# Transposing fetches of the experts' token rows, woven back from two planes of 16-bit halves

## The reference

```
o = (silu(x @ gate_e.T) * (x @ up_e.T)) @ down_e.T      # 256 -> 128 -> 256 channels
out = x2 + gb * (sum over the 6 experts of weight * o  +  a shared expert of width 256)
```

## Time and profile before

| | us |
|---|---|
| median of 3 runs (lowest, highest) | 1335.8 (1335.38, 1337.43) |
| the profiled execution's own time | 1335.87 |
| its span, first to last instruction | 1334.1 |
| TensorE busy in the span | 1283.5 |
| VectorE busy | 1070.0 |
| ScalarE busy | 759.0 |
| GpSimd busy | 650.2 |

### The profile page before, as it was taken

How to read it: one execution, slowest core, us unless ns; L and a number is a source line. 1 busy time by engine, 2 the same in 40 slices (tenths; PEclk the granted TensorE clock), 3 DMA queues, 4 the chain that set the end, 5 groups by cost and what they waited for, 6 DMA issues and landing times.

```text
span 1334.1 us, 26082 instructions
## 1 busy us (share of the span) xinstructions
PE 1283.5 (96%) x8098; PEld 637.6 (48%) x8098; DVE 1070.0 (80%) x2592; ACT 759.0 (57%) x1093; POOL 650.2 (49%) x964
## 2 busy tenths in 40 slices
PE   9996999999999999999999999999999999999895
PEld 6652322333323323323333232558888888885441
DVE  6878999999999999999999996475444566665497
ACT  4553777777676776777677768314444444446100
POOL 1004123335655755656466557756766655564100
PEclk8996999999999999999999999999999999999998
DMA  6777555534347256264363453768776665554798
GB/s 219 242 232 192 148 154 109 96 74 115 88 110 172 54 136 143 68 144 111 93 162 80 145 183 101 244 220 264 235 218 201 192 185 183 183 172 131 292 327 322
DMA packets 215235, 224.81 MB, mean 169 GB/s; under 512 B 109926, under 2 KB 177142, under 8 KB 214972
## 3 DMA queue, kind: packets, MB, share of 16 engines
q1 hardware_dynamic: 188524, 150.22, 41.9%
q0 software_dynamic: 21152, 66.10, 14.1%
q10 hardware_dynamic: 5424, 6.82, 1.5%
HBM read 127.33 MB, written 95.70 MB: 167 GB/s over the span
## 4 chain that ended last, share of the span: by engine, by line
PE 69%; DVE 10%; DMA 4%; POOL 4%; SPq 2%; issue 1%; ACT 1%; ACTq 0%; DVEq 0%; POOLq 0%
PE psO L1381 14%; PE psE L1368 13%; PE psM L1358 9%; PE ex_psGU L1969 7%; PE ex_psGU L2030 7%; DVE piece_max L1236 6%; PE ex_psY L2050 4%; PE ex_psY L1979 3%; DMA wide<-results 2%; PE psM L576 2%; PE ex_psX L2016 2%; PE ex_psX L1957 2%; SPq L144 2%; PE co_psS L2446 1%; PE psGU L1721 1%
## 5 line engine op out<-in xcount | busy, mean ns | idle before, releaser
L1236 DVE TENSOR_REDUCE piece_max<-psM 128x1 f32<-128x512 f32 x1008 | 631.0, 682 | 20.0 <-PE psM L1358 16.5
L1319 ACT ACTIVATE wide<-psE 128x1024 f32<-128x1024 f32 x512 | 497.1, 1021 | 186.9 <-PE psE L1368 184.6
L1368 PE MATMUL psE<-wide 49*128 49x512 bf16 (+1 forms) x2048 | 327.3, 379 | 5.0 <-DMA wide<-maxima 4.7
L1358 PE MATMUL psM<-wide 48*128 48x512 bf16 x1008 | 312.0, 389 | 11.7 <-DVE piece_max L1236 11.5
L1381 PE MATMUL psO<-wide 128*32 128x512 f32 x2048 | 273.2, 606 | 0.6 <-ACT wide L1319 0.6
L2261 POOL DMA_INDIRECT results<-vals_inv,places x208 | 200.3, 963 | 127.7 <-DVE vals_inv L2142 104.5
L1358 PEld LDWEIGHTS psM<-wide 48*128 48x128 bf16 x1008 | 76.4, 93 | 322.9 <-DVE piece_max L1236 271.4
L1368 PEld LDWEIGHTS psE<-wide 49*128 49x128 bf16 (+1 forms) x2048 | 118.0, 95 | 94.5 <-issue 11.9
L1455 POOL DMA_INDIRECT lists<-last_rows,slot x96 | 93.8, 977 | 52.6 <-issue 22.3
L1455 POOL DMA_INDIRECT lists<-rows,slot x96 | 94.6, 986 | 49.4 <-PE psO L1381 26.4
L2030 PE MATMUL ex_psGU<-wide,ex_xT 128*128 (+1 forms) x416 | 107.8, 382 | 0.8 <-ACT h2T L2103 0.8
(11 more groups left out here) (349 smaller groups left out, 1570.8 us busy)
## 6 DMA issues: line engine op xcount, KB each, us to landing
wide<-qk_parts SPq DMA_DIRECT2D x384, 64.0 KB, 2.7
wide<-results SPq DMA_DIRECT2D x16, 1536.0 KB, 9.8
qk_parts<-parts SPq DMA_DIRECT2D x32, 384.0 KB, 2.7
rows<-lists SPq DMA_DIRECT2D x26, 320.0 KB
h2Ts<-lists SPq DMA_DIRECT2D x26, 320.0 KB
xin<-in_x_dram SPq DMA_DIRECT2D x16, 512.0 KB, 4.0
wide<-in_guT_dram SPq DMA_DIRECT2D x3, 2560.0 KB, 9.9
rows<-lists SPq DMA_DIRECT2D x44, 160.0 KB
```

What stands on the lines that cost most here:

```text
L1236: v.tensor_reduce(piece_max[:, qh, (x * PAIRS + h) * KT // QH + qt, kh:kh + 1], bank_of("piece", PIECES * group + n), AX.X, ALU.max, negat ...
L1319: nc.scalar.activation(probs[:, step % 2, 2 * pair:2 * pair + 2], psE[:, pair], ACT.Exp, scale=HD ** -0.5).then_inc(exp_ok, 1)
L1358: nc.tensor.matmul(bank_of(*user), qa[g][rows, h, qt * P:(qt + 1) * P], ka[g][rows, h, kh * 512:(kh + 1) * 512], start=True, stop=True).th ...
L1368: mm = nc.tensor.matmul(psE[:, pair, x], k[g][part, pair, kt * P:(kt + 1) * P], q[g][part, pair, qh * 512:(qh + 1) * 512], start=(q is qa) ...
```

## The change

1. `env.lists` keeps each token's 256 channels as two planes of 16-bit halves: 256 upper halves, then 256 lower halves. ScalarE makes them per chunk with two copies of 128x1024 16-bit elements (`planes`, at w = `SPLIT` = 25 of the window, and once in the closing stage); the normalised tokens stay in `env.xhat`, from which `turn_half` now reads. GpSimd's scatter waits for `planes_ok`, and SyncE's next load of values into the same memory waits for the transposes and the planes.
2. In the expert stage SyncE fetches the planes with a transposing DMA (`dma_start_transpose`), so that channels lie on partitions, and the 64 words of weights and positions with a plain DMA behind it: two transfers for each pair or tile, four for a mixed tile.
3. TensorE's transposes of rows (`turn_pair`, and those of `body`) are gone, and `ex_psX` with them.
4. The halves are woven into `ex_xT` by copies whose output steps over every second 16-bit place. In pairs ScalarE writes the upper halves and VectorE the lower ones (128x512 each); for single and mixed tiles ScalarE writes both (two of 128x256).
5. SyncE waits for the weaving (`x_ok`, `low_ok`) where it waited for the transposes (`x_done`).

The core of the diff:

```
-PROJECT, TURN, GATE, PLACE = 11, 21, 23, 28
+PROJECT, TURN, GATE, SPLIT, PLACE = 11, 21, 23, 25, 28
...
+def planes(act, env, c):
+    act.wait_ge(env.h2_ok, c + 1)
+    if c > 1:
+        act.wait_ge(env.scattered[(c - 2) % CPB], 16 * TPC * TOPK * ((c - 2) // CPB + 1))
+    halves = env.xhat.bitcast(U16).rearrange("p i (d h) -> p i d h", h=2)
+    to = env.rows_of(c)[:, :, 0:D].bitcast(U16)
+    env.nc.scalar.activation(to[:, :, 0:D], halves[:, :, :, 1], ACT.Copy)
+    env.nc.scalar.activation(to[:, :, D:2 * D], halves[:, :, :, 0], ACT.Copy).then_inc(env.planes_ok, 1)
...
-                    wait(sp, env.h2_ok, c)
+                    wait(sp, env.turned, KC * c)
+                    wait(sp, env.planes_ok, c)
...
             def scatter_step_by_step(c):
+                pool.wait_ge(env.planes_ok, c + 1)
...
             def pair_of_tiles(t, u, row):
-                wait(sp, x_done, t - DEEP + 2)
+                wait(sp, x_ok, t - DEEP + 2)
+                wait(sp, low_ok, min(t - DEEP + 2, SURE))
                 wait(sp, dest_ok, t - DEEP + 2)
-                sp.dma_start(pair_rows[u // 2], env.lists[bass.ds(row, 2 * P)].rearrange("(j p) n -> p j n", p=P)
+                sp.dma_start_transpose(pair_planes[u // 2], in_planes[bass.ds(row, 2 * P), 0:2 * D]).then_inc(rows_in[u], 16)
+                sp.dma_start(pair_marks[u // 2], env.lists[bass.ds(row, 2 * P), D:ROW].rearrange("(j p) n -> p j n", p=P)
                              ).then_inc(rows_in[u], 16)
...
-                for half, row in enumerate(both):
-                    sp.dma_start(rows[u][half * HALF:(half + 1) * HALF], env.lists[bass.ds(row, HALF)]
+                for half, row in enumerate(of_halves):
+                    sp.dma_start_transpose(tile_planes[u][:, :, half * HALF:(half + 1) * HALF],
+                                           in_planes[bass.ds(row, HALF), 0:2 * D]).then_inc(rows_in[u], 16)
+                    sp.dma_start(marks[u][half * HALF:(half + 1) * HALF], env.lists[bass.ds(row, HALF), D:ROW]
                                  ).then_inc(rows_in[u], 16)
...
-            def turn_pair(p, v):
-                wait_pair_rows(pe, p, v)
-                wait(pe, x_ok, 2 * p - 2)
-                for j in range(2):
-                    for k in range(KC):
-                        mm = nc.tensor.transpose(psX[:, v % 2, (2 * k + j) * P:(2 * k + j + 1) * P],
-                                                 rows[2 * v + j][:, k * P:(k + 1) * P], env.ident[:])
-                mm.then_inc(x_done, 2)
...
             def copy_pair(p, v):
-                act.wait_ge(x_done, 2 * p + 2)
+                wait_pair_rows(act, p, v)
+                if p == 0:
+                    act.wait_ge(env.closing_y_done, env.closing_chunks)
                 wait(act, gu_done, 2 * p - 2)
-                nc.scalar.activation(xT[:, v % 2], psX[:, v % 2], ACT.Copy).then_inc(x_ok, 2)
+                to = xT[:, v % 2].bitcast(U16).rearrange("p (n t h) -> p n t h", n=KC, h=2)
+                nc.scalar.activation(to[:, :, :, 1], pair_planes[v][:, 0:KC], ACT.Copy).then_inc(x_ok, 2)
...
             def body(t, u):
                 if exists(t):
-                    act.wait_ge(x_done, t + 1)
+                    wait_rows(act, t, u)
                     wait(act, gu_done, t - 1)
-                    nc.scalar.activation(xT[:, u % 2, 0:D], psX[:, u % 2, 0:D], ACT.Copy).then_inc(x_ok, 1)
+                    to = xT[:, u % 2, 0:D].bitcast(U16).rearrange("p (n t h) -> p n t h", n=KC, h=2)
+                    nc.scalar.activation(to[:, :, :, 1], tile_planes[u][:, 0:KC], ACT.Copy)
+                    nc.scalar.activation(to[:, :, :, 0], tile_planes[u][:, KC:2 * KC], ACT.Copy).then_inc(x_ok, 1)
...
             def pairs(p, v, h):
-                dve.wait_ge(x_done, 2 * p + 2)
+                wait_pair_rows(dve, p, v)
+                if p == 0:
+                    dve.wait_ge(env.closing_y_done, env.closing_chunks)
+                wait(dve, gu_done, 2 * p - 2)
+                to = xT[:, v % 2].bitcast(U16).rearrange("p (n t h) -> p n t h", n=KC, h=2)
+                nc.vector.tensor_copy(to[:, :, :, 0], pair_planes[v][:, KC:2 * KC]).then_inc(low_ok, 2)
```

More of the change, by code:

```diff
@@ L11 @@
 I32 = mybir.dt.int32
+U16 = mybir.dt.uint16
 AX = mybir.AxisListType
@@ L1307, in beside @@
                     half_scores(act, env, c, bank_of(c, w))
+                if c >= 0 and pair == 1 and w == SPLIT:
+                    planes(act, env, c)
             for n in range(HALF_PIECES):
@@ L1446, in pad @@
 def pad(eng, env, end):
-    eng.dma_start(env.lists[bass.ds(end, HALF)], env.pad_row[0:HALF]).then_inc(env.pads_out, 16)
+    eng.dma_start(env.lists[bass.ds(end, HALF)], env.pad_row[0:HALF].bitcast(I32)).then_inc(env.pads_out, 16)
 def scatter_chunk(nc, env, c, first=0, end=TPC * TOPK):
@@ L1536, in _ @@
             pool.wait_ge(env.routed, 1)
+            pool.wait_ge(env.planes_ok, LAST + 1)
             scatter_chunk(nc, env, LAST, 0, EARLY_LISTS)
@@ L1564, in _ @@
             half_scores(act, env, LAST, psGP[:])
+            planes(act, env, LAST)
             gate_shared(3, 1)
@@ L1799, in expert_phase @@
             "p (u n) -> p u n", n=ROW)
-        rows = [(env.rows if u < TPC else spare_rows)[:, u % TPC] for u in range(DEEP)]
-        pair_rows = [(env.rows if u < TPC else spare_rows)[:, u % TPC:u % TPC + 2] for u in range(0, DEEP, 2)]
+        both = [(env.rows if v < HALVES // 2 else spare_rows)[:, 2 * v % TPC:2 * v % TPC + 2].rearrange("p u n -> p (u n)")
+                for v in range(HALVES)]
+        pair_planes = [both[v][:, 0:2 * D].bitcast(U16).rearrange("p (n t) -> p n t", n=2 * KC) for v in range(HALVES)]
+        tile_planes = [both[u // 2][:, u % 2 * D:(u % 2 + 1) * D].bitcast(U16).rearrange("p (n t) -> p n t", n=2 * KC)
+                       for u in range(DEEP)]
+        pair_marks = [both[v][:, 2 * D:2 * ROW].rearrange("p (j n) -> p j n", j=2).bitcast(I32)
+                      for v in range(HALVES)]
+        marks = [pair_marks[u // 2][:, u % 2] for u in range(DEEP)]
+        in_planes = env.lists.bitcast(U16)
         xT = sb("ex_xT", [P, 2, KC * 2 * P])
@@ L2011, in body @@
                     window[:] = words_in(pe, tile_words)
-                if exists(t):
-                    wait_rows(pe, t, u)
-                    wait(pe, x_ok, t - 1)
-                    for k in range(KC):
-                        mm = nc.tensor.transpose(psX[:, u % 2, k * P:(k + 1) * P], rows[u][:, k * P:(k + 1) * P],
-                                                 env.ident[:])
-                    mm.then_inc(x_done, 1)
                 if exists(t - 1):
@@ L2128, in dest @@
             def dest(u, h, *which):
-                both = rows[u][:, D:ROW].rearrange("p (k e) -> p k e", k=2)
+                both = marks[u].rearrange("p (k e) -> p k e", k=2)
                 for part, e in zip((slice(0, P),) if len(which) == 1 else (slice(0, HALF), slice(HALF, P)), which):
                     copy = nc.vector.tensor_copy(pair[part, DEEP * h + u].unsqueeze(2),
-                                                 both[part, :, bass.ds(e, 1)].bitcast(I32))
+                                                 both[part, :, bass.ds(e, 1)])
                 copy.then_inc(dest_ok, 1)
@@ L2506, in declare @@
     env.h2T_d = dram("turned", (LAST - 1, P, KC, CH), F32)
-    env.lists = dram("lists", (LIST_ROWS, ROW), F32)
+    env.lists = dram("lists", (LIST_ROWS, ROW), I32)
     env.table_d = dram("tile_table", (2 * P, 2), I32)
@@ L2575, in declare_routing @@
         "table_out", "sfc_ok", "wrec_ok", "slot_ok", "slot_read", "bent_turned", "picked", "helped"))
+    env.planes_ok = env.sem("rt_planes_ok")
     env.h2T_of = lambda c: env.h2T[:] if c < LAST else env.xin[:].rearrange("p i d -> p (i d)").rearrange("p (k t) -> p k t", k=KC)
```

51 lines of the change are left out of this document (26 added, 25 removed).

## The result

The changed kernel takes 1439.91 us (median of 4 runs, 1439.16 to 1442.26) beside 1336.62 us (1335.38 to 1337.58) for the kernel before: a ratio of 1.0794, 95% interval 1.0776 to 1.0813. It is slower by 103 us, where 38 us less were forecast. The profiled execution took 1442.26 us, its span is 1440.4 us.

The account below looks back on a forecast made before the run. TensorE was taken to bound the expert stage. Pairs 18.2 + single tiles 19.2 + mixed tiles 2.3 - planes 2.0 = 37.7 us off 1335.9 us gave 1298 us; range 1289 to 1345.

Parts of the forecast that it names:

- the one on SyncE's queue: Expert stage: SyncE's issues stay at 1.4 of 2.59 us per pair; dearest issue of a like size 3.12 us.
- a gain of 19.2: 88 single tiles: removing TensorE's transposes saves 0.218 us each, 19.2 us in all.
- ScalarE's 2.08: Mixed tiles: ScalarE sets the pace at 2.08 us, over TensorE's 2.01, so 16 tiles give 2.3 us.
- SyncE's issue: Rival, SyncE's queue: issue grows with the pieces; at 3.12 us a pair takes 4.2 us; chance 0.03 (above 3 us).
- TensorE, 45.6 us to be had: Expert stage: transposes removed from TensorE, 22.9 + 19.2 + 3.5 us, the most the change can bring.
- the term of 18.2 us: Pairs: 52 steps fall from 3.03 to 2.68 us, 0.35 us each, 18.2 us.
- The DMA engines: Expert stage: a pair costs them 2.47 us of the 2.59 available, 95%; a single tile 1.11 of 1.41.
- Short landings: Rival, expert stage: DMA engines pay per landing piece, a pair takes 4.07 us; 1415 us in all; chance 0.10.
- Transfers in series: Rival, expert stage: a transposing transfer starts only when the one before has landed; some 1460 us; chance 0.06.
- Weaving: Copies into ex_xT: pairs 0.62 us on ScalarE and 0.6 on VectorE; single tiles 0.38 us per ScalarE copy of 256.
- GpSimd, "no loss but little margin": Expert stage: GpSimd's sends take 2.52 us per pair, barely under 2.59; no loss counted.
- planes: Attention and closing stage: two added ScalarE copies, 2.04 us each time, cost about 0.3 us per chunk, 2 us in all.

Follow-up runs that it names:

- experiment 3: Changed kernel with only pairs fetched by transposing transfers; single and mixed tiles by plain ones, their transposition left out: 1341.22 us, ratio 1.0047.
- experiment 11: As 10 (pairs by transposing DMA, other tiles plain with 16-bit TensorE transposes), but 28 pads issued from ScalarE's queue instead of SyncE's: 1326.54 us, ratio 0.9935.
- 10: Changed kernel with pairs still transposed by DMA, single and mixed tiles by plain fetches and four 16-bit TensorE transposes per tile: 1348.32 us, ratio 1.0101.
- experiment 1: Changed kernel with all planes fetched by plain transfers, as many as before, the transposition left out: 1320.84 us, ratio 0.9897.
- experiment 5: Changed kernel fetching only the plane of upper halves, half the bytes, and weaving it twice; on another chip: ratio 1.0540.
- experiment 2: Changed kernel with each marks transfer issued a second time, to a place nobody reads: 1532.06 us, ratio 1.1481.
- 4: Changed kernel with only single and mixed tiles fetched by transposing transfers; pairs by plain ones, their transposition left out: 1416.26 us, ratio 1.0610.

## Why the prediction was wrong, step by step

**The step that failed is the one on SyncE's queue:** "With the nearest, 0.49 for the transposing one, 0.38 for the marks and 0.5 for a pad stay at 1.4 of 2.59 us." A transposing issue costs 1.29 us in the pairs. But that alone, 1.29 + 0.42 + 0.52 = 2.2, would still fit 2.59. Two terms were left out: the address work between issues, 0.2 us each and 0.4 to 0.6 per pair, and the loads of registers, some 1.1 us per four pairs without pads and 2.1 with them. Both stood in the trace of before as gaps and loads that cost nothing there, since SyncE was waiting anyway. Together that is 3.15 us per pair and more while the pads last (the timeline of experiment 3), and taking the pads away gives 20 us of the pairs back (experiment 11 against 10).

**The range of that step was applied to the pairs only.** Its upper bound, 3.12 us, came from the rows, and it was asked from what price on a pair no longer fits. The single tile was never put to the same sum: it has the tightest time, 1.41 us, and the same two issues. At 1.20 + 0.42 + 0.4 + a quarter for its loads it doesn't fit by far, and already bare issues of 0.49 + 0.38 with 0.4 and 0.25 beside them would have come to 1.5. This is where 71 of the 106 us are: the prediction had them at a gain of 19.2. For the mixed tiles the step had "four issues at 0.47, 1.9 us, below ScalarE's 2.08"; plain they take 2.66 and 0.5 for loads (experiment 1 had 2.84 per tile, a part of it met by slack), transposing 3.87.

**The rival "SyncE's issue" was the right mechanism** in place and kind, but it was made to grow "with the pieces" and given 0.03. It hardly grows: for 64, 128 or 256 rows of 512 columns the medians lie between 1.17 and 1.31 us, and half the columns take 0.01 to 0.02 off a tile's (the rows of after, experiment 5). Its price at 3.12 us is also added up wrongly: 3.12 + 0.38 + 0.5 is 4.0 us per pair, not 4.2. A fixed price is mild for the largest transfer and ruinous for the smallest, the reverse of what the rival had.

**TensorE, 45.6 us to be had:** right as a bound. Where SyncE was relieved the pairs came down from 3.03 to 2.71 (experiment 1) and 2.74 us (11), against 2.68 forecast; the term of 18.2 us was 15.9 and 14.8. Single tiles at 1.48 without SyncE's long issues, against 1.41.

**The DMA engines:** 95% of 2.59 us was forecast for the pairs. The row shows 0.92 x 3.09 = 2.84 us of work per pair, more than 2.47; at 2.74 us per pair (11) the share reads 1.06, over what can be, so shares near 1 aren't to be taken to the hundredth. Short landings are refuted: at 4.07 us per pair experiment 11 would be impossible. Transfers in series are refuted too, though their 1460 us came nearest to the measured 1440: that is luck. They had 2.3 us for a single tile and 6.0 for a mixed one; within a round tiles are issued every 2.04 us and their gate and up products begin 2.0 to 2.1 us apart (1104.82, 1106.95, 1108.91), the mixed tiles take 3.87, and an issue more that transposes nothing costs 92 us (experiment 2). The rate of the Trainium skill's page "DMA: Bandwidth & Descriptors" (Latency and other measured facts), by which a pair would take 1.0 us, was not measured here; the runs agree with it only in that the transfers' landings are 2% of the chain after. The 1309 ns for one block in its page "VectorE: DVE Perf Modes" (The three transpose paths) are near what SyncE pays here per instruction, 1.16 to 1.31 us, but for 4 to 8 blocks at once; taken as a price per issue, they would have given 88 x (1.31 + 0.42 + 0.40 + 0.21 - 1.65) = 61 us on the single tiles (0.21 is an eighth of a load).

**Weaving:** right for the pairs in sum (ScalarE 0.78 us where 0.62 was taken, VectorE 0.46 where 0.6 was), low for the single tiles:

```profile
L2118 ACT ACTIVATE ex_xT<-rows x52: 481/489/496, 1067.7 to 1326.7; 128x256 uint16<-128x256 uint16 x52
```

0.49 against 0.38 us. It was hidden: the chains of experiments 1, 3, 4 and 11 give the writes of ex_xT at most 1.5% wherever they name them. Whether ScalarE would set the pace of the mixed tiles at 2.08 us stays open, as SyncE is later in every run that fetches a mixed tile by four transfers. Copies with two-byte stepping output cost ScalarE a quarter more than the 4-byte rows, not twice.

**GpSimd, "no loss but little margin":** the margin is used up once the pairs run at 2.7 us (experiment 11), as the rows had it. **planes:** the last product of the closing stage's shared expert starts at 902.3 instead of 899.9 us, 2.4 later, with 2.0 forecast. A further 2.1 us go from there to the first down product, counted at 0; in experiments 3, 10 and 11, which fetch the first pairs in the same way, that stretch is 1.4 us shorter to 0.3 longer than before, so it may be spread between executions.

## What to carry to other kernels

A queue that issues transfers is an engine with a time budget: count all it executes per tile (issues, address arithmetic, register loads, pads), from two successive issues without a wait between them, and hold the sum against the tightest tile, not the largest. An operation that the trace has never shown should be bounded by a fixed price as well as by one that grows with size. Transfers of a dear fixed price should be few and large: here the transposing fetch pays for a pair, once the queue is rid of its pads (139.5 us in experiment 11 against 154.3), and not for a tile (216.2 us against 145.1).

## What the runs showed of the hardware

- A transposing DMA costs SyncE 1.17 to 1.31 us of issue (medians) for 64 to 256 rows of 512 two-byte columns, and 1.16 to 1.17 for 64 or 128 rows of 256; a plain issue of the same rows' marks takes 0.42 to 0.47 us, about a third. The DMA engines carried a transposing fetch of 256 rows every 2.74 us beside the other traffic (experiment 11).
- Loads of values into SyncE's registers cost about 0.2 us for each value (4: 0.86, 8: 1.67, 16: 3.6 us), and joining them saves nothing. The Trainium skill's page "Runtime: NRT & Kernel Launch" (Instruction fetch mechanics) has about 200 ns per register even in bulk, and the trace agrees on SyncE. It does not agree on ScalarE's queue, where four values took 0.31 us, from the tile pad_slot, from which SyncE's loads of three or four take 0.70 in the median.
- TensorE's granted clock fell to a mean of 0.92 and 0.67 of full in stretches where it was busy 76% and 66% of the time and waited between tiles; 0.67 means two thirds of the stretch at 1.2 GHz and the rest at 2.4. By the profile's busy time it then spends 136.75 / (180 / 2.46) = 1.87 us on a single tile, against 1.63 before, though it has two transposes less. Only a part of this can be the clock: from 1100 to 1120 us, at a granted clock of 1.00, it is still 14.62 / (20 / 2.33) = 1.70. It costs nothing here, as SyncE is later still.
- Between two chips the same kernel took 1334 and 1454 us, and the changed one (with wide loads) 1.080 and 1.057 times as long, so even ratios carry over only roughly.
